# Attention strips loaded straight into the query and key tiles, the first group's one stage early, and products on idle TensorE whose results nobody reads

## The chip, the core and the metric

The kernel runs on one core of a Trainium2 chip, as one program. The metric is device time in microseconds (us), the median of several executions. The core has four compute engines, each with its own instruction queue: TensorE (PE, matrix products; PEld in the rows is its loading of weights), VectorE (DVE), ScalarE (ACT) and GpSimd (POOL). SyncE (SP) only issues DMAs here; ACT and POOL can issue them too. SBUF is the on-chip memory of 128 partitions, PSUM the eight banks into which TensorE writes. TensorE's clock has two levels, 1.2 and 2.4 GHz; the profile shows the granted clock as a share of the upper one (0.50 or 1.00).

## The reference

4096 tokens (8 sequences of 512) of width 128 pass through six residual steps. The part that the change touches is the fifth, windowed attention with 16 heads of width 8, and the mixture of experts before and after it:

```python
x = x + 0.5 * _L0_ffn_ref(_layernorm(x), ...)     # 8 experts, top 2
x = x + _L0_attn_ref(_layernorm(x), ...)          # a selective scan (Mamba)
x = x + 0.5 * _L0_ffn_ref(_layernorm(x), ...)
x = x + 0.5 * _L1_ffn_ref(_layernorm(x), ...)     # shared + 8 routed experts, top 1
x = x + _L1_attn_ref(_layernorm(x), ...)          # below
x = x + 0.5 * _L1_ffn_ref(_layernorm(x), ...)

def _L1_attn_ref(x, Wqkv, bqkv, Wout, bout):      # H = 16, WIN = 64, d = 8
    qkv = (x @ Wqkv.T + bqkv).reshape(B, S, 3, H, d).transpose(2, 0, 3, 1, 4)
    ...
    scores = jnp.einsum('bhncd,bhnld->bhncl', qc, kb) / np.sqrt(d)
    scores = jnp.where(band, scores, -jnp.inf)    # each query sees 64 keys
    attn = jax.nn.softmax(scores, axis=-1)
    o = jnp.einsum('bhncl,bhnld->bhncd', attn, vb)
    ...
    return o @ Wout.T + bout
```

## The kernel before

**Stages.** The program is a row of blocks with a barrier of all engines after each: `front` (the first three steps, woven together), `ffn1` with the tag `_f1`, `attention` (names ending in `_a`), and `ffn1` again with the tag `_f1b`. The residual stream stays in SBUF as `x_all`. In each block every engine has one instruction list, written out in Python and kept in that order; semaphores carry the dependences between engines.

**Products of high and low parts.** Operands are split into a part rounded to fp32r (`_hi`) and the rest (`_lo`), and `three` sums the three products that matter (L118 to L120 in the rows).

**ffn1.** A shared expert runs over 32 slots J (4 for each sequence): `shared_up` (six products into two PSUM banks), Gelu on ACT (`gel`, L1845), a multiplication on DVE (`hf`, L1854), `shared_down` two slots later (L1834). `EJ` = 24 slots come at the start, together with normalizing (`xn`), transposing (`xT`, L114), the gate (L1735) and the routing of each sequence; then 40 tiles of routed tokens; then the last slots, J from 24 to `AJ` - 1 = 31. The first block (`_f1`) also gets `opening`, functions of the attention stage that are run in it for sequence 0: loading the attention's weights, its norm, the transpose and the products for query, key and value (steps "T", "q", "k", "v" of `prep_pe`, `prep_act`, `prep_dve`), and the stores of queries and keys.

**Attention.** For each sequence the query and key, with their high and low parts, are written to DRAM (`q_rows`, `k_rows`: four copies of 8 rows for each head), so that a load can bring 32 rows, one head's products of both parts, under each other. A group is four heads (128 rows); there are 4 groups for each sequence, n = 0 to 31. `strips` loads a group's rows into `k_strips` and `q_strips`, two buffers each. ACT then copies the queries into `qd[n % 3]` (`set_queries`, four copies of 32 partitions), a tile in which each head's 32 rows have their own columns and the rest is zero, so that one product gives four heads' scores; DVE copies the keys into `kT[n % 3]` (`set_keys`). A query tile holds, for each block b of 32 queries, the 128 columns (head, query) next to each other:

```python
qd = [sb(f"qd{r}", [P, NB, HG, QB], F32R) for r in range(RQ)]
x = eng.matmul(BS[c][:, j * KW:(j + 1) * KW], qd[n % RQ][:, b, :, :].rearrange("p r q -> p (r q)"), kT[n % RQ][:, b * QB:b * QB + KW], ...)
```

The first operand of a product is the one that is loaded as weights, the second is streamed: a query block is the weights of a score product, 96 keys are streamed. A unit u is half a group, 8 blocks: there are 64. Each goes through `scores` (PE), `mask` and `find_max` (DVE), `less_max` (POOL), `exps` (ACT), `turn` (transposes on PE), `copy_p` (ACT), `weigh` (PE), `normalize` (DVE), `keep_own` (POOL) and `gather` (PE). PE runs them skewed: at turn t of its loop come `scores(t + 2)`, `turn(t)`, `weigh(t - 1)` and `gather(t - 2)`, and between them the steps that prepare the next sequence, by the table PLACES.

**Order at the start of attention.** PE waits for the first query and key tile; its order is `scores` of units 0, 1 and 2, the transpose "T" of sequence 1, then `turn(0)`. "T" needs `norm_out(1)` on ACT, and that `norm_root(1)` on POOL. POOL first sets all three `qd` tiles and the edges of `kT` to zero.

## Time and profile before

| | us |
|---|---|
| median of 3 executions | 1939.84 (1930.39 to 1942.37) |
| profiled execution, its device time | 1927.48 |
| its span, first to last instruction | 1925.7 |
| mean granted TensorE clock in it | 0.973 |
| block `_f1` begins | 1129.8 |
| block `attention` begins | 1367.2 |
| block `_f1b` begins | 1691.8 |

The span is the time in which the trace's rows lie, counted from 0. Most rows below are of the timeline: start, duration, engine, line, operation, output and inputs, count, and in brackets the idle time of the engine before it with what ended it. Rows of stretches give, for each engine, its busy time and number of instructions, then the granted clock (a share of the full one), the busy share of the 16 DMA engines and GB/s. "x16" with one duration means 16 instructions that follow one another.

### The profile page before, as it was taken

The page shows a single profiled execution, that of the slowest core. Times are in us where ns is not written, and L with a number is a line of the kernel's source. Part 1 is how long each engine was busy: PE and PEld are TensorE (multiplying, and loading weights), DVE is VectorE, ACT ScalarE, POOL GpSimd, SP SyncE. Part 2 cuts the span into 40 slices and gives each one's busy share as a digit, 9 for nine tenths or more (in the row PEclk, how much of TensorE's full clock was granted, in tenths as well). Part 3 has the DMA queues.
Part 4 walks back from the last instruction along what each step waited for, and adds up shares of the span by engine and source line. Part 5 has one row for each costly group of instructions (what it writes and reads, how often), then busy time and mean ns, then how long its engine had stood idle before and what let it go on. Part 6 is the DMA issues. An engine that isn't in the chain of part 4 may idle for free. (4 is left out here: it accounts for less than half of the span.)

```text
span 1925.7 us, 35660 instructions
## 1 busy us (share of the span) xinstructions
PE 1752.5 (91%) x12117; PEld 1506.5 (78%) x12117; DVE 1250.3 (65%) x2930; ACT 1103.0 (57%) x1935; POOL 1210.9 (63%) x1201
## 2 busy tenths in 40 slices
PE   7999898999999999887689989999699999989998
PEld 6878676787877778766477878888599999978886
DVE  2358789778787787978886436433567666656433
ACT  3466665766666766565555554343577767553442
POOL 3228687776877768778895725464656555534664
PEclk9999999999999999999889989999799999989999
DMA  4023332332333223332221401112554354101113
GB/s 145 1 69 113 92 107 87 108 97 86 102 91 109 94 84 108 91 101 78 78 99 55 117 14 44 38 46 67 156 160 127 116 154 137 39 24 35 46 45 108
DMA packets 120638, 166.95 MB, mean 87 GB/s; under 512 B 13878, under 2 KB 55820, under 8 KB 120460
## 3 DMA queue, kind: packets, MB, share of 16 engines
q1 hardware_dynamic: 112716, 147.74, 25.2%
q0 software_dynamic: 7168, 15.87, 2.7%
q8 instruction: 101, 1.65, 0.3%
q10 hardware_dynamic: 576, 1.05, 0.2%
q14 instruction: 77, 0.63, 0.1%
HBM read 114.28 MB, written 50.33 MB: 85 GB/s over the span
## 5 line engine op out<-in xcount | busy, mean ns | idle before, releaser
L777 POOL TENSOR_TENSOR db<-du_m,bt 128x512 f32<-128x512 f32 x256 | 328.5, 1284 | 137.6 <-DVE bank L782 136.7
L782 DVE TENSOR_TENSOR_SCAN bank<-bank,db 128x512 f32<-128x512 f32 x256 | 312.5, 1221 | 20.1 <-ACT bank L767 19.9
L808 POOL TENSOR_TENSOR y_m<-y_m,ph 128x512 f32<-128x512 f32 x240 | 313.4, 1307 | 0.4 <-DVE ph L797 0.4
L767 ACT ACTIVATE bank<-dt_m,a_neg 128x512 f32<-128x512 f32 x256 | 176.2, 688 | 96.6 <-DVE ph L797 90.0
L797 DVE TENSOR_TENSOR ph<-bank,ct 128x512 f32<-128x512 f32 x240 | 165.9, 691 | 11.2 <-POOL y_m L808 3.2
L1241 POOL TENSOR_TENSOR s_a<-s_a,mx_a 128x768 f32<-128x768 f32 x64 | 94.2, 1472 | 88.3 <-DVE mx_a L1349 88.2
L1380 PE MATMUL bank<-vb_a,pT_a 96*128 96x64 f32 x1024 | 121.5, 272 | 0.2 <-DVE o_a L1391 0.2
L1380 PEld LDWEIGHTS bank<-vb_a,pT_a 96*128 96x128 f32 x1024 | 119.4, 192 | 0.3 <-DVE o_a L1391 0.3
L354 PEld LDWEIGHTS bank<-dn,hf2b 128*128 128x128 f32 x680 | 91.3, 196 | 15.4 <-DVE x_all L413 5.7
L354 PEld LDWEIGHTS bank<-dn,hf1b 128*128 128x128 f32 x680 | 89.8, 193 | 11.2 <-DVE x_all L413 2.9
L354 PE MATMUL bank<-dn,hf2b 128*128 128x128 f32 x680 | 92.1, 280 | 6.5 <-DVE x_all L413 4.7
L354 PEld LDWEIGHTS bank<-dn,hf0b 128*128 128x128 f32 x688 | 90.3, 192 | 9.3 <-DVE x_all L413 1.0
L354 PEld LDWEIGHTS bank<-dn,hf2a 128*128 128x128 f32 x680 | 89.6, 193 | 8.5 <-DVE x_all L413 1.3
L354 PEld LDWEIGHTS bank<-dn,hf0a 128*128 128x128 f32 x688 | 90.3, 192 | 7.5
L354 PEld LDWEIGHTS bank<-dn,hf1a 128*128 128x128 f32 x680 | 89.0, 191 | 8.0 <-DVE x_all L413 0.6
L354 PE MATMUL bank<-dn,hf1b 128*128 128x128 f32 x680 | 90.7, 277 | 2.4 <-DVE x_all L413 2.0
L354 PE MATMUL bank<-dn,hf0b 128*128 128x128 f32 x688 | 91.1, 275 | 1.0 <-DVE x_all L413 0.6
L354 PE MATMUL bank<-dn,hf0a 128*128 128x128 f32 x688 | 90.8, 275 | 0.0
L354 PE MATMUL bank<-dn,hf2a 128*128 128x128 f32 x680 | 90.4, 276 | 0.4 <-DVE x_all L413 0.3
L354 PE MATMUL bank<-dn,hf1a 128*128 128x128 f32 x680 | 89.7, 275 | 0.2 <-DVE x_all L413 0.2
L385 ACT ACTIVATE hf1a<-bank,b 128x512 f32<-128x512 f32 x85 | 58.2, 685 | 53.6 <-PE bank L120 53.3
L1311 ACT CAST qd_a<-q_strips_a 32x512 fp32r<-32x512 f32 x128 | 78.7, 615 | 15.6 <-DMA q_strips_a<-q_rows 14.5
(458 smaller groups left out, 4864.9 us busy)
## 6 DMA issues: line engine op xcount, KB each, us to landing
bt<-bc_rows SPq DMA_DIRECT2D x128, 256.0 KB, 3.5
ct<-bc_rows SPq DMA_DIRECT2D x128, 256.0 KB, 3.4
sorted<-zero_row SPq DMA_DIRECT2D x64, 288.0 KB, 3.9
k_strips_a<-k_rows SPq DMA_DIRECT2D x32, 256.0 KB, 3.0
q_strips_a<-q_rows SPq DMA_DIRECT2D x32, 256.0 KB, 3.9
q_rows<-q_hi_a SPq DMA_DIRECT2D x16, 256.0 KB, 3.0
q_rows<-q_lo_a SPq DMA_DIRECT2D x16, 256.0 KB, 3.4
vb_a<-v_rows SPq DMA_DIRECT2D x16, 240.0 KB, 3.9
```

Of the source, the lines that this page charges most:

```text
L354: x = eng.matmul(Y.psum[:, t], hf[r][:, t], W["dn"][:, e, c, :], start=c == 0 and k == 0, stop=c == HC - 1 and k == NT - 1, skip_group_che ...
L385: eng.activation(hf[v % NR][:], HB[hbank(v)].psum[:], ACT.Relu, bias=W["b1"][:, e, c:c + 1]).then_inc(relu.sem)
L767: eng.activation(DH[J % 2][:], dt[s % 2][:, j % NH, :], ACT.Exp, scale=a_neg[:, j % NH, j // NH:j // NH + 1]).then_inc(da_done.sem)
L777: eng.tensor_tensor(db[J % RD][:], du[s % 2][:, j % NH, :], bt[N % RB][:], ALU.mult).then_inc(db_done.sem)
L782: eng.tensor_tensor_scan(DH[J % 2][:], DH[J % 2][:], db[J % RD][:], 0.0, ALU.mult, ALU.add).then_inc(hs_done.sem)
L797: eng.tensor_tensor(out, DH[J % 2][:], ct[N % RB][:], ALU.mult).then_inc(ph_done.sem)
L808: eng.tensor_tensor(y[s % 2][:, j % NH, :], y[s % 2][:, j % NH, :], ph[J % RP][:], ALU.add).then_inc(ys_done.sem)
L1241: eng.tensor_tensor(X[:], X[:], M[:, :, None].to_broadcast([P, UB, KW]), ALU.subtract).then_inc(sub_done.sem)
L1311: x = eng.copy(qd[n % RQ][p, :, r, :], q_strips[n % 2][p, :].rearrange("p (b q) -> p b q", q=QB))
L1380: x = eng.matmul(BO[:, at:at + 2 * GD], pT[u % 2][:, c * BB + j, :], vb[s % 2][:, b:NB + 1:NB - b, g * GD:(g + 1) * GD], start=True, stop= ...
```

## The change

1. **No copies into the tiles.** `q_strips`, `k_strips`, `set_queries` and `set_keys` go. `strips` now loads keys (one DMA of 128 partitions) and queries (four DMAs of 32 partitions, one for each head) straight into `kT[n % 3]` and `qd[n % 3]`; it waits until the scores of group n - 3 are done.
2. **Another layout of the queries.** Each head's queries are written in the order (query in block, block), so that a row stays contiguous for the DMA. The 128 weights of a score product are now every 16th element of 2048, 64 bytes apart, and ACT and DVE write the query parts with that stride (`by_block`).
3. **Sequence 0 is prepared one slot earlier** in `_f1`: "T", "q" and "k" move from slots J = 30, 31, 32 to 29, 30, 31. Its stores are split between ACT (high keys) and SP (the rest), and the first group's strips are loaded in `_f1`, into tiles whose memory `ffn1` no longer uses then; POOL zeroes them there (`clear_group(0)`).
4. **POOL's order at the start of attention** changes: group 1's tile, `vb`, `less_max(0)`, group 2's tile, `norm_root(1)`, `less_max(1)`, `bias_out(0)`.
5. **Products that nobody reads** (`warm`, 128 x 512 each, into a free bank): 8 at the start of each `ffn1` and 7 more after its first transposes, 24 at the end of `_f1`, 4 at the start of attention.

```diff
+def warm(eng, psum, tile, n):
+    for _ in range(n):
+        eng.matmul(psum[:], tile[:, 0, 0:P], tile[:, 0, :], start=True, stop=True)
...
         def prep_act(eng, s, name):
...
-                eng.activation(hi[:], X[:], ACT.Identity, bias=b_cols[:, col:col + 1]).then_inc(pa.sem)
+                eng.activation(by_block(hi, name), X[:].rearrange("p (b q) -> p b q", q=QB), ACT.Identity, bias=b_cols[:, col:col + 1]).then_inc(pa.sem)
...
+        def by_block(tile, name):
+            return tile[:].rearrange("p (q b) -> p b q", b=NB) if name == "q" else tile[:].rearrange("p (b q) -> p b q", q=QB)
...
+        def strips(eng, s, g, keys=True, heads=range(HG)):
+            n = s * HG + g
+            if g == 0:
+                eng.wait_ge(q_out.sem, q_out.at(s, "last"))
+                eng.wait_ge(k_out.sem, k_out.at(s, "last"))
+            q, ld = qd[n % RQ], strip_in[n % RQ]
+            if n >= RQ:
+                eng.wait_ge(sc_done.sem, sc_done.at(2 * (2 * (n - RQ) + 1) + 1))
+            else:
+                eng.wait_ge(zeroed.sem, zeroed.at(0, f"qd{n}"))
+            if keys:
+                eng.dma_start(kT[n % RQ][:, PAD:PAD + SEQ].bitcast(F32), k_rows[s, HG * g:HG * g + HG].rearrange("r c d t -> (r c d) t")).then_inc(ld.sem, 16)
+            for h in heads:
+                eng.dma_start(q[32 * h:32 * h + 32, h, :].bitcast(F32), q_rows[s, HG * g + h].rearrange("c d t -> (c d) t")).then_inc(ld.sem, 16)
...
-            eng.dma_start(k_strips[n % 2][:], k_rows[s, heads].rearrange("r c d t -> (r c d) t")).then_inc(strip_in[n % 2].sem, 16)
-            eng.dma_start(q_strips[n % 2][:], q_rows[s, heads].rearrange("r c d t -> (r c d) t")).then_inc(strip_in[n % 2].sem, 16)
...
-                x = eng.matmul(BS[c][:, j * KW:(j + 1) * KW], qd[n % RQ][:, b, :, :].rearrange("p r q -> p (r q)"), kT[n % RQ][:, b * QB:b * QB + KW], start=True, stop=True)
+                x = eng.matmul(BS[c][:, j * KW:(j + 1) * KW], qd[n % RQ][:].rearrange("p h (q b) -> p (h q) b", b=NB)[:, :, b], kT[n % RQ][:, b * QB:b * QB + KW], start=True, stop=True)
...
@@ ffn1: sync, act @@
             if opening:
                 opening["store_queries"](eng, 0)
+                opening["store_low_keys"](eng, 0)
+                opening["strips"](eng, 0, 0, heads=(0, 1))
...
             if opening:
-                for name in ("q", "k"):
-                    opening["prep_act"](eng, 0, name)
-                opening["store_keys"](eng, 0)
+                opening["prep_act"](eng, 0, "k")
+                opening["store_high_keys"](eng, 0)
+                opening["strips"](eng, 0, 0, keys=False, heads=(2, 3))
...
@@ ffn1: pe @@
+            warm(eng, HB[3].psum, up_hi[0], 8)
...
                 turns(v)
+                if v == -1:
+                    warm(eng, HB[3].psum, up_hi[0], 7)
                 gates(v)
...
-                if opening and J >= AJ - 2:
-                    opening["prep_pe"](eng, 0, ("T", "q", "k", "v")[J - AJ + 2])
+                if opening and J in (AJ - 3, AJ - 2, AJ - 1, AJ + 1):
+                    opening["prep_pe"](eng, 0, {AJ - 3: "T", AJ - 2: "q", AJ - 1: "k", AJ + 1: "v"}[J])
+            if opening:
+                HB[0].wait(eng)
+                warm(eng, HB[0].psum, up_hi[0], 24)
```

How this moves instructions is seen at three places. The first is ACT at the end of `_f1` and the start of attention; `gel_f` are the last slots' Gelus. Before:

```order
L1845 ACTIVATE gel_f<-bank 128x512 [waits f1_shared_up,f1_shared_hidden]
L1175 ACTIVATE q_hi_a<-bank,b_cols_a 128x512 [waits a_prep_pe,a_bias_dve]
L1175 ACTIVATE k_hi_a<-bank,b_cols_a 128x512 [waits a_prep_pe,a_bias_dve]
L1075 DMA k_rows<-k_hi_a 16x8x512 [waits a_prep_dve]
L1075 DMA k_rows<-k_hi_a 16x8x512
L1075 DMA k_rows<-k_lo_a 16x8x512 x2
L2090 UNCONDITIONAL_BRANCH
L1492 UNCONDITIONAL_BRANCH [waits barrier_Pool_Activation_PE_DVE_SP_release]
L1311 CAST qd_a<-q_strips_a 32x16x32 [waits a_strips0_in,a_zeroed]
```

Now:

```order
L1188 ACTIVATE q_hi_a<-bank,b_cols_a 128x16x32 [waits a_prep_pe,a_bias_dve]
L1847 ACTIVATE gel_f<-bank 128x512 [waits f1_shared_up,f1_shared_hidden]
L1188 ACTIVATE k_hi_a<-bank,b_cols_a 128x512 [waits a_prep_pe,a_bias_dve]
L1079 DMA k_rows<-k_hi_a 16x8x512 [waits a_prep_act]
L1079 DMA k_rows<-k_hi_a 16x8x512
L1216 DMA qd_a<-q_rows 32x512 [waits a_zeroed,a_k_stored,a_q_stored]
L1216 DMA qd_a<-q_rows 32x512
L2097 UNCONDITIONAL_BRANCH
L1490 UNCONDITIONAL_BRANCH [waits barrier_Pool_Activation_PE_DVE_SP_release]
L1359 ACT_TABLE_LOAD
```

The query's high part has moved ahead of the last Gelu, two of the key stores have gone to SP, and two strip loads, which wait for all stores, now stand before the barrier; the copies after it are gone. The second place is POOL at the start of attention. Before (`s_a` is the `less_max` of units 0 to 3):

```order
L1256 MEMSET qd_a 128x2048 x3
L87 TENSOR_SCALAR sd_a<-mv_a 128x4 [waits a_norm_dve]
L96 TENSOR_SCALAR nm_a<-mv_a 128x4
L90 TENSOR_TENSOR rs_a<-sd_a,minus_half 128x4 [waits a_norm_pool]
L100 TENSOR_TENSOR nm_a<-nm_a,rs_a 128x4 [waits a_norm_pool]
...
L1236 TENSOR_TENSOR x_all<-x_all,b_all_a 128x512 [waits a_bias_dve,a_prep_act]
L1241 TENSOR_TENSOR s_a<-s_a,mx_a 128x768 [waits a_max_done] x4
```

Now:

```order
L1223 MEMSET qd_a 128x2048
...
L1271 TENSOR_TENSOR s_a<-s_a,mx_a 128x768 [waits a_max_done]
L1221 MEMSET kT_a 128x32
L1222 MEMSET kT_a 128x32
L1223 MEMSET qd_a 128x2048
L87 TENSOR_SCALAR sd_a<-mv_a 128x4 [waits a_norm_dve]
L96 TENSOR_SCALAR nm_a<-mv_a 128x4
L90 TENSOR_TENSOR rs_a<-sd_a,minus_half 128x4 [waits a_norm_pool]
```

The norm of sequence 1 (`rs_a`, `nm_a`) stood ahead of the first `less_max` and now stands behind it and behind one more zeroing. The third is PE at the same border (L1834, now L1836, is `shared_down`). Before:

```order
L1154 MATMUL bank<-xT_a,w_k_a 128x512 [waits a_prep_act]
L1834 MATMUL bank<-k_dn,hf_f 128x128 [waits f1_shared_hidden]
L1834 MATMUL bank<-k_dn,hf_f 128x128 x3
L1158 MATMUL bank<-w_v_a,xT_a 128x128 [waits a_prep_dve]
L1158 MATMUL bank<-w_v_a,xT_a 128x128 x3
L2090 UNCONDITIONAL_BRANCH
L1494 UNCONDITIONAL_BRANCH [waits barrier_Pool_Activation_PE_DVE_SP_release]
L1335 MATMUL bank<-kT_a,qd_a 128x96 [waits a_keys_set,a_queries_set]
```

Now:

```order
L1163 MATMUL bank<-xT_a,w_k_a 128x512 [waits a_prep_act]
L1836 MATMUL bank<-k_dn,hf_f 128x128 [waits f1_shared_hidden]
L1836 MATMUL bank<-k_dn,hf_f 128x128 x3
L1836 MATMUL bank<-k_dn,hf_f 128x128 [waits f1_shared_hidden]
L1836 MATMUL bank<-k_dn,hf_f 128x128 x3
L1167 MATMUL bank<-w_v_a,xT_a 128x128 [waits a_prep_dve]
L1167 MATMUL bank<-w_v_a,xT_a 128x128 x3
L120 MATMUL bank<-k_up_hi 128x512 [waits f1_shared_hidden]
L120 MATMUL bank<-k_up_hi 128x512 x23
L2097 UNCONDITIONAL_BRANCH
L1492 UNCONDITIONAL_BRANCH [waits barrier_Pool_Activation_PE_DVE_SP_release]
L120 MATMUL bank<-k_up_hi 128x512 x4
```

The key product stands one `shared_down` (two rows) earlier, and 24 + 4 unread products stand on the two sides of the barrier.

## Rows read from the trace of the kernel before

**Rows 1.** The page, busy time of TensorE: share of the span, instructions.

```profile
PE 1752.5 (91%) x12117; PEld 1506.5 (78%) x12117; DVE 1250.3 (65%) x2930; ACT 1103.0 (57%) x1935; POOL 1210.9 (63%) x1201
```

**Rows 2.** Stretches: the attention once it runs.

```profile
1390.00:1660.00 270.00, 267.27 (x2847) 252.91 (x2847) 188.77 (x451) 194.46 (x331) 153.06 (x156) 1.00 0.46 137
```

**Rows 3.** All waits of PE from 1384 to 1660 us: total, times, longest.

```profile
PE bank L1289 <- ACT oT_a L1296: 2.7, 7, 0.4
```

**Rows 4.** Timeline, attention, one unit: scores, turn, the next scores.

```profile
1663.85 0.97 PEld L1335 LDWEIGHTS bank<-kT_a,qd_a 128*128 128x128 f32 x8
...
1664.76 0.83 PEld L1361 LDWEIGHTS bank<-ident,s_a 128*96 128x96 f32 x8
...
1668.12 0.97 PEld L1335 LDWEIGHTS bank<-kT_a,qd_a 128*128 128x128 f32 x8
```

**Rows 5.** Timeline, `_f1`: streamed products of 512 columns at clock 1.00.

```profile
1342.49 0.39 PE L118 MATMUL bank<-xT_hi_f,k_up_hi 128*128 128x512 f32 x1
...
1342.72 0.40 PE L119 MATMUL bank<-xT_lo_f,k_up_hi 128*128 128x512 f32 x1
```

**Rows 6.** The page, groups by cost: busy, mean ns, idle before them.

```profile
L1311 ACT CAST qd_a<-q_strips_a 32x512 fp32r<-32x512 f32 x128 | 78.7, 615 | 15.6 <-DMA q_strips_a<-q_rows 14.5
```

**Rows 7.** Timeline, the end of `_f1`: the low part of the keys.

```profile
1359.21 0.74 DVE L1184 SCALAR_TENSOR_TENSOR k_lo_a<-bank,b_cols_a,k_hi_a 128x512 fp32r<-128x512 f32 x1
```

**Rows 8.** Stretches: the border to attention, and where the clock is back.

```profile
1362.00:1364.00 2.00, 0.00 (x0) 0.00 (x0) 0.00 (x0) 0.00 (x0) 0.00 (x0) 0.98 0.95 290
...
1384.00:1386.00 2.00, 2.00 (x12) 1.46 (x12) 1.33 (x3) 1.98 (x5) 0.58 (x1) 0.90 0.00 0
```

**Rows 9.** Timeline, the start of attention.

```profile
1367.22 0.34 SPq L1206 DMA_DIRECT2D k_strips_a<-k_rows  x1
...
1367.52 5.57 POOL L1256 MEMSET qd_a<- 128x2048 f32 x3
...
1370.73 2.50 ACT L1311 CAST qd_a<-q_strips_a 32x512 fp32r<-32x512 f32 x4 [12.35 <-DMA q_strips_a<-q_rows]
...
1373.18 0.23 POOL L87 TENSOR_SCALAR sd_a<-mv_a 128x4 f32<-128x4 f32 x1
1373.28 3.59 PEld L1335 LDWEIGHTS bank<-kT_a,qd_a 128*128 128x128 f32 x16 [12.31 <-ACT qd_a L1311]
...
1374.80 0.20 POOL L100 TENSOR_TENSOR nm_a<-nm_a,rs_a 128x4 f32<-128x4 f32 x1
...
1377.06 1.46 POOL L1241 TENSOR_TENSOR s_a<-s_a,mx_a 128x768 f32<-128x768 f32 x1
...
1379.31 1.63 ACT L104 ACTIVATE xn_a<-x_all,nm_a,rs_a 128x128 f32<-128x128 f32 x4
...
1381.12 0.71 PEld L114 LDWEIGHTS bank<-ident,xn_a 128*128 128x128 f32 x4
```

**Rows 10.** Stretches: the start of `_f1`.

```profile
1132.00:1140.00 8.00, 6.11 (x19) 4.85 (x19) 2.39 (x8) 4.62 (x9) 3.54 (x20) 0.50 0.09 25
```

**Rows 11.** Timeline, the start of `_f1` on TensorE.

```profile
1131.52 0.89 PE L114 MATMUL bank<-ident,xn_f 128*128 128x128 f32 x4 [3.17 <-ACT xn_f L1756]
...
1134.30 0.79 PE L118 MATMUL bank<-xT_hi_f,k_up_hi 128*128 128x512 f32 x1 [1.89 <-DVE xT_lo_f L1778]
...
1141.92 0.25 PEld L118 LDWEIGHTS bank<-xT_hi_f,k_up_hi 128*128 128x128 f32 x1
```

**Rows 12.** Timeline, the start of `_f1b` on TensorE.

```profile
1693.48 1.12 PE L114 MATMUL bank<-ident,xn_f1b 128*128 128x128 f32 x4 [2.72 <-ACT xn_f1b L1756]
...
1696.49 0.79 PE L118 MATMUL bank<-xT_hi_f1b,k_up_hi 128*128 128x512 f32 x1 [1.89 <-DVE xT_lo_f1b L1778]
...
1697.08 0.63 PE L119 MATMUL bank<-xT_lo_f1b,k_up_hi 128*128 128x512 f32 x1
...
1697.51 0.63 PE L120 MATMUL bank<-xT_hi_f1b,k_up_lo 128*128 128x512 f32 x1
...
1705.45 0.39 PE L118 MATMUL bank<-xT_hi_f1b,k_up_hi 128*128 128x512 f32 x1
```

More of the change, by code:

```diff
@@ L1070, in store_queries, with store_high_keys, store_low_keys @@
                 eng.dma_start(q_rows[s, :, copy, :, :], (q_hi, q_lo)[copy % 2][:].bitcast(F32)).then_inc(q_out.sem, 16)
-        def store_keys(eng, s):
+        def store_high_keys(eng, s):
+            eng.wait_ge(pa.sem, pa.at(s, "k"))
+            for copy in (0, 1):
+                eng.dma_start(k_rows[s, :, copy, :, :], k_hi[:].bitcast(F32)).then_inc(k_out.sem, 16)
+        def store_low_keys(eng, s):
             eng.wait_ge(pd.sem, pd.at(s, "k"))
-            for copy in range(4):
-                eng.dma_start(k_rows[s, :, copy, :, :], (k_hi, k_lo)[copy // 2][:].bitcast(F32)).then_inc(k_out.sem, 16)
+            for copy in (2, 3):
+                eng.dma_start(k_rows[s, :, copy, :, :], k_lo[:].bitcast(F32)).then_inc(k_out.sem, 16)
         def load_weights(eng):
@@ L1183, in prep_dve @@
                 eng.wait_ge(pa.sem, pa.at(s, name))
-                eng.scalar_tensor_tensor(lo[:], X[:], b_cols[:, col:col + 1], hi[:].bitcast(F32), ALU.add, ALU.subtract).then_inc(pd.sem)
+                eng.scalar_tensor_tensor(by_block(lo, name), X[:].rearrange("p (b q) -> p b q", q=QB), b_cols[:, col:col + 1],
+                                         by_block(hi, name).bitcast(F32), ALU.add, ALU.subtract).then_inc(pd.sem)
             elif name == "v":
@@ new lines, in clear_group @@
+        def clear_group(eng, r):
+            eng.memset(kT[r][:, 0:PAD].bitcast(F32), 0.0)
+            eng.memset(kT[r][:, PAD + SEQ:].bitcast(F32), 0.0)
+            eng.memset(qd[r][:].bitcast(F32), 0.0).then_inc(zeroed.sem)
+        with ExitStack() as ahead:
+            tiles = [[ahead.enter_context(nc.sbuf_tensor(f"{name}{r}_a", [P, *shape], F32R)) for name, shape in (("qd", (HG, SEQ)), ("kT", (PADDED,)))]
+                     for r in range(RQ)]
+        qd, kT = [t[0] for t in tiles], [t[1] for t in tiles]
@@ L1190, in attention @@
+        yield dict(load_weights=load_weights, store_queries=store_queries, store_high_keys=store_high_keys, store_low_keys=store_low_keys, strips=strips, clear_group=clear_group, set_ones=set_ones, set_masks=set_masks, biases_pe=biases_pe, biases_dve=biases_dve,
                    norm_stats=norm_stats, norm_root=norm_root, norm_out=norm_out, prep_pe=prep_pe, prep_act=prep_act, prep_dve=prep_dve)
-        qd = [sb(f"qd{r}", [P, NB, HG, QB], F32R) for r in range(RQ)]
-        kT = [sb(f"kT{r}", [P, PADDED], F32R) for r in range(RQ)]
@@ L1194, in attention @@
-        q_strips, k_strips = two("q_strips", [P, SEQ]), two("k_strips", [P, SEQ])
+        sb("groups", [P, RQ * (HG * SEQ + PADDED)])
         vb = two("vb", [KW, NB + 1, D])
@@ L1212, in sync @@
                     store_queries(eng, s)
-                    store_keys(eng, s)
-                eng.wait_ge(q_out.sem, q_out.at(s, "last"))
-                eng.wait_ge(k_out.sem, k_out.at(s, "last"))
-                strips(eng, s, 0)
+                    store_high_keys(eng, s)
+                    store_low_keys(eng, s)
+                    strips(eng, s, 0)
                 strips(eng, s, 1)
@@ L1250, in pool @@
         def pool(eng):
-            for r in range(RQ):
-                eng.memset(kT[r][:, 0:PAD].bitcast(F32), 0.0)
-                x = eng.memset(kT[r][:, PAD + SEQ:].bitcast(F32), 0.0)
-            x.then_inc(zeroed.sem)
-            for r in range(RQ):
-                eng.memset(qd[r][:].bitcast(F32), 0.0).then_inc(zeroed.sem)
-            norm_root(eng, 1)
+            clear_group(eng, 1)
             for p in range(2):
@@ L1262, in pool @@
             x.then_inc(zeroed.sem)
+            less_max(eng, 0)
+            clear_group(eng, 2)
+            norm_root(eng, 1)
+            less_max(eng, 1)
             bias_out(eng, 0)
-            for u in range(2):
-                less_max(eng, u)
             for t in range(NU + 1):
@@ L1405, in pe @@
         def pe(eng):
+            warm(eng, BT[0], K["up_hi"][0], 4)
             for u in range(2):
@@ L1449, in act @@
                             prep_act(eng, s + 1, name)
-                if t % 2 == 0 and t + 4 < 2 * NG:
-                    set_queries(eng, t // 2 + 2)
             project_act(eng, NSEQ - 1)
@@ L1477, in dve @@
                             prep_dve(eng, s + 1, name)
-                if t % 2 == 0 and t + 4 < 2 * NG:
-                    set_keys(eng, t // 2 + 2)
                 if k == 4 and 1 <= s < NSEQ:
@@ L2074, in dve @@
             for J in range(EJ, AJ + 2):
+                if opening and J in (AJ - 1, AJ):
+                    opening["prep_dve"](eng, 0, ("q", "k")[J - AJ + 1])
                 if J < AJ:
@@ L2080, in dve @@
                     opening["biases_dve"](eng)
-                if opening and J == AJ - 4:
+                if opening and J == AJ - 5:
                     eng.wait_ge(added.sem, added.at(FINAL.index(0)))
                     opening["norm_stats"](eng, 0)
-                if opening and J == AJ:
-                    opening["prep_dve"](eng, 0, "q")
             if opening:
-                for name in ("k", "v"):
-                    opening["prep_dve"](eng, 0, name)
+                opening["prep_dve"](eng, 0, "v")
         with nc.Block() as block:
```

46 lines of the change are left out of this document (9 added, 37 removed).

## The prediction

> **What bounds the kernel now.** I read the page first: TensorE is busy for 91% of the span [rows 1], more than any other engine, so the question at each place is whether TensorE waits there. Then the stretches and the waits of the attention. Once it runs, TensorE is busy for 267.27 of 270 us at a clock of 1.00 [rows 2], and all that it waits for is 2.7 us behind a copy of ACT [rows 3]. ACT and DVE are busy for 194 and 189 of those 270 us: they have room. So time that is taken from ACT or DVE there buys nothing, and time that is added to a product is paid in full. The reader is to see in [rows 4] how such a unit passes: 8 score products start at 1663.85, the transposes at 1664.76, the next unit's scores at 1668.12, a period of 4.27 us with no gap.
>
> TensorE does wait at the borders of the stages, so I read these in the timeline. At the start of attention it waits for 12.31 us until the first strips are in their tiles [rows 9]. And behind each border its clock is low: 0.50 from 1132 to 1140 [rows 10], and still 0.90 on average in 1384 to 1386, 17 us after attention began [rows 8]. There products take about twice as long: 0.43 us from 1697.08 to 1697.51 against 0.23 us at clock 1.00 [rows 12, 5].
>
> **The copies (nothing).** 128 copies on ACT, 78.7 us [rows 6], and 32 on DVE go. All but the first group's stand beside a TensorE that does not wait, so they return nothing; at most the 2.7 us of [rows 3], which are waits for another copy of ACT. In their place come 160 DMAs instead of 64 on SP's queue, for the same bytes. They wait for the scores of group n - 3 and are needed two groups, 4 units or 17 us, later. A first strip load took 3.5 us from issue to use (1367.22 to 1370.73, [rows 9]); with five issues of some 0.4 us it is 5 to 6. Also behind a sequence's eight stores it has about three units, 13 us. That cover hides it; without it each group would add up to 5 us, 160 us in all, and I see nothing that takes the cover away.
>
> **The strided weights (0, up to +55 us).** Each of the 512 score products now loads 128 weights that lie 64 bytes apart. No row shows a strided weight load, so I bound it by its neighbours. Contiguous, 8 products take 0.91 us [rows 4], 0.114 each. They stream only 96 columns, which at the rate of [rows 5] (0.23 us for 512) is 0.043 us: the loading of weights sets their pace, at 0.89 ns a weight. The streamed side passes an element in 0.45 ns, so that reading of SBUF can go twice as fast as weights are loaded. If the stride halves the fastest reading, weights still come at 0.90 ns and the cost is nil. If it halves the weights' own rate, each load costs another 0.107 to 0.114 us: 512 x 0.107 = +55 us, with nothing to hide it. Below nothing there is no case: the same 128 weights are loaded. I take 0, because the weight load uses half the rate that the streamed rows show, and keep +55 as the far end.
>
> The Trainium skill has a rule against this layout (SBUF — State Buffer, section Door 1: The DMA port swizzle): SBUF lines are 16 bytes, full speed needs at least two hits in a line, and an access that goes to a new line each time pays a penalty. Here every weight is in a line of its own; before, four shared one. The page gives no size of the penalty, and no row of this trace shows it; by the rule the sum is that of the second rival, without it the forecast's.
>
> ACT and DVE write the query parts with the same stride, 8 times each. Bounded by a doubling of about 0.7 us each this is 11 us of work on engines with room; on the path it stands once, for sequence 0, +0 to +1.4 us.
>
> **The start of attention (-1.7 us, from -5 to +2).** Sequence 0's keys come one slot earlier. A slot is some 2.3 us (six products at 0.23 and four f32 products of about the same together), but the low keys wait on DVE and ACT for the last Gelu and the query's part now, so I take 1.9: the low part ends at 1358.1 instead of 1359.95 [rows 7]. The stores are bound by the DMA engines (share 0.95 at 290 GB/s, [rows 8]), all eight start 1.9 us earlier, and so have landed by about 1365.2 instead of 1367.1. Then come the strips, 3.5 us, and no copy of 2.50 us: scores may begin at 1368.7 instead of 1373.28, -4.6 us. But scores are not what TensorE is late for. It becomes busy for good with the transpose "T" at 1381.12, and ahead of it stands now a longer chain. From the first score to POOL's start on unit 0 it was 3.8 us at most (1373.28 to 1377.06, with another operation of POOL ahead), I take 3.3 from 1368.7, to 1372.0; POOL's `less_max(0)` 1.46, to 1373.5; zeroing of a tile 5.57/3 = 1.86 and its edges 0.2, to 1375.5; `norm_root(1)` 1373.18 to 1375.00, 1.82, to 1377.3; `norm_out(1)` on ACT 1.63, to 1379.0; "T" at 1379.1. That is -2.0. If the barrier waits for ACT's own strip loads to land (before, it opened when the last store must have landed), attention begins at 1368.8, DVE has its norm statistics to do first, and "T" comes at 1379.8, -1.3. I take the middle, -1.7. What is late next is thus POOL's chain, not the strips. The bounds: -5 if the strips alone counted; +2 if a strided write, the barrier and POOL all go against it.
>
> The 24 products at the end of `_f1` take 24 x 0.23 = 5.5 us from 1359.2 and end before the barrier opens, so they cost nothing. I give them nothing either: before, the clock was 0.98 on average in 1362 to 1364 [rows 8] after the last weight load at 1361.0 (1373.28 less the 12.31 idle), so it fell near 1364; now it may hold until about 1367.5, and between then and "T" TensorE has long gaps again (two units of scores are 1.9 us of work). The time in which it came back, 1381 to 1385, stays.
>
> **The start of `_f1` (-3.0 us, from -4 to 0).** TensorE is free from 1129.8; its transposes come at 1131.52 [rows 11]. Eight products of 0.23 us end at 1131.7, so they delay it by 0.1 to 0.2. Seven more end at 1134.0, before the first real product at 1134.30. If TensorE is thus busy enough, the clock doesn't fall, and the work from 1134.30 to 1141.92 (12 products of `three`, 8 of the gate, 4 transposes) passes at clock 1.00: 12 x 0.23 + 8 x 0.11 = 3.7 us against 7.6. But the transposes there need ACT's `gel` and `xn`, 2.3 us behind the first six products, at about 1138.2, so that the next slot begins at 1138.7 instead of 1141.92: -3.2, less the 0.2. TensorE is then busy without waits to speak of, so what is gained stays.
>
> **The start of `_f1b` (-1.8 us, from -3 to +2.5).** Here the clock is low when the block begins at 1691.8. Eight products at 0.43 us end at 1695.2, and the transposes, ready at 1693.48 [rows 12], wait for them: +1.7. The seven end at 1698 to 1699.1, and the first real product moves from 1696.49 by 1.7 to 2.6. In return the clock rises earlier. Before, it was back by 1705.45, 9.0 us after dense work began. Dense work now begins at 1691.8, so it is back by 1700.8, or by 1697 if the some 4 us of attention (1381.12 to 1385) hold. Real work done at 1705.45 was worth 4.5 us at clock 1.00; now it is done at 1704.4 or 1702.7: -1.0 or -2.7, middle -1.8.
>
> **Sum.** 0 + 0 - 1.7 - 3.0 - 1.8 = -6.5 us on the profiled execution (1927.48 to 1921.0). That execution lies 12.4 us below the median of the three runs; the same difference from the median, 1939.84, is 1933.3. The runs lie 12 us apart: about 1% is what a measurement of this kernel can tell from no change.
>
> **Rivals.** (a) *The clock isn't held.* The unread products don't keep or bring back the clock, as in `_f1b`, where it stayed low through 8 us of dense work. Then only their delays are left: +0.2 in `_f1`, +2.6 in `_f1b`, and -1.7 in attention: +1.1, 1941. For it: the same 8 us. Against it: it did come back in each case, and in `_f1` it need only not fall. Chance 0.2. (b) *Strided weights are slow*, slower than before: one mechanism, at L1341, 512 times. It decides from 0.05 us a load (26 us less the 6.5 of the rest is +1%); at +0.107 it gives 1939.8 + 55 - 6.5 = 1988. For it: the products are bound by loading weights, and nothing covers it [rows 2, 4]. Against it: the rate of [rows 5]. Chance 0.15, with half of it below 1965. (c) *ACT and DVE were the hidden bound.* If relief brings TensorE's products closer together, by 0.3 us in each of 64 units, it is -19 and more, 1914. Against it stands [rows 3]. Chance 0.04.
>
> **How the numbers follow.** Forecast 0.61, (a) 0.2, (b) 0.15, (c) 0.04. Within 1%: 0.81, the first two. Slower: 0.15. Faster by over 1%: 0.04. The forecast alone spans 1939.8 - 12 to 1939.8 + 4.5 by its bounds, some 5 us more on each side for the scatter of the medians. The range goes from 1921 to 1958: it leaves out (c) below, and the larger part of (b) above.
>
> **What would show it.** In the attention stretch: PEld pitch of L1341 at 0.114 us and a unit of 4.27 us; if it is 5.1 us, (b). At the start: first scores near 1368.7, then a gap of TensorE, ended by "T", whose releaser is ACT's `xn_a` and behind it POOL; if "T" comes before 1377, my chain is wrong. In `_f1`: clock 1.00 from 1132 to 1140 and the third slot near 1138.7. In `_f1b`: transposes near 1695.2, clock back by 1700. What would make the prediction wrong: a price on the strided weights, strips that land late in the middle of attention (TensorE waits for a strips DMA at L1341), or a barrier that holds attention back.

## The result: 152 us slower, and the profile after

The changed kernel takes 2091.31 us (median of 4 runs, 2083.93 to 2097.41) against 1938.99 for the kernel before (4 runs beside them): a ratio of 1.0791, with a 95% interval of 1.0740 to 1.0842. The forecast was 1933 us, and its range ended at 1958. In the experiments below one execution of e10 (4690 us) and one of e12 (3442 us) stand far off all others of their kernels and count in none of the medians and ratios. The profiled execution has a span of 2087.2 us, 161.5 more than the 1925.7 of before.

The page of the kernel after: the busy time, the line of granted clocks in 40 slices, and two groups of weight loads.

```profile
PE 1924.9 (92%) x12175; PEld 1668.8 (80%) x12175; DVE 1246.6 (60%) x2898; ACT 1037.3 (50%) x1807; POOL 1206.6 (58%) x1201
...
PEclk9999999999999999989999999986556666599999
...
L1386 PEld LDWEIGHTS bank<-vb_a,pT_a 96*128 96x128 f32 x1024 | 177.0, 268 | 0.7 <-DVE o_a L1397 0.3
...
L1341 PEld LDWEIGHTS bank<-kT_a,qd_a 128*128 128x128 f32 x512 | 117.2, 310 | 5.7 <-DMA qd_a<-q_rows 1.6
```

TensorE is as busy as in [rows 1], 92%, with 58 products more, and yet for 172 us longer. The clock line shows where: nine slices in the attention stand at 5 to 8 tenths. It is not only the scores (L1341) that got dearer: L1386, the weighing of values, whose weights did not change their place, went from 192 to 268 ns a load. From the start of the first scores to the start of the last eight it is now 459.8 us (1370.1 to 1829.9) against 299.1 (1373.3 to 1672.4): 160.7 us, the whole loss.

Stretches of the kernel after (busy us of PE, PEld, DVE, ACT and POOL, then the granted clock), to be held against [rows 2]:

```profile
1400.00:1500.00 100.00, 100.00 (x677) 95.45 (x676) 42.83 (x100) 32.31 (x53) 35.10 (x38) 0.64 0.28 80
1500.00:1700.00 200.00, 200.00 (x1344) 187.27 (x1345) 90.01 (x204) 65.81 (x105) 70.86 (x74) 0.66 0.31 90
...
1564.00:1580.00 16.00, 16.00 (x150) 15.00 (x148) 8.80 (x16) 7.08 (x12) 6.14 (x6) 0.99 0.66 201
1584.00:1624.00 40.00, 40.00 (x237) 37.99 (x237) 15.53 (x44) 11.39 (x19) 13.69 (x16) 0.50 0.13 37
```

TensorE never waits here, 100.00 of 100 us, and its clock is nevertheless 0.50, the lower level of 1.2 GHz, for most of the time: a mean of 0.65 between 1.00 and 0.50 means 70% of the time at 0.50. It changes about once in a sequence of 8 units: some 40 us low, some 16 us high. The copies that are gone freed ACT and DVE; nothing came of it.

The timeline of TensorE at either level (start, duration, one row for a run of like products):

```profile
1481.18 2.00 PE L1341 MATMUL bank<-kT_a,qd_a 128*128 128x96 f32 x8
1482.98 1.93 PE L1367 MATMUL bank<-ident,s_a 128*96 128x128 f32 x8
...
1489.14 2.00 PE L1341 MATMUL bank<-kT_a,qd_a 128*128 128x96 f32 x8
...
1506.54 1.96 PE L1341 MATMUL bank<-kT_a,qd_a 128*128 128x96 f32 x8
1508.33 1.12 PE L1315 MATMUL bank<-w_o_a,oT_a 128*128 128x128 f32 x8
```

Take starts, not durations. At clock 1.00 eight scores take 1.79 us (1506.54 to 1508.33), twice the 0.91 of [rows 4]. At 0.50 they take 1.80 (1481.18 to 1482.98), nearly what contiguous weights took at that clock ([rows 9], 3.59 us for 16). So the time of these loads, 64 bytes apart, does not follow TensorE's clock. A whole unit at 0.50 is 7.96 us (1481.18 to 1489.14).

### The profile page after: what moved, and what is told of

It is laid out like the page before. It is cut to its first block and busy times, and to the rows that moved or that the text cites. A ratio compares the mean times of both kernels' runs of the same rounds, so it can differ in the third digit from the quotient of the medians.

```text
span 2087.2 us, 35618 instructions
## 1 busy us (share of the span) xinstructions
PE 1924.9 (92%) x12175; PEld 1668.8 (80%) x12175; DVE 1246.6 (60%) x2898; ACT 1037.3 (50%) x1807; POOL 1206.6 (58%) x1201
## 5 line engine op out<-in xcount | busy, mean ns | idle before, releaser
L1386 PEld LDWEIGHTS bank<-vb_a,pT_a 96*128 96x128 f32 x1024 | 177.0, 268 | 0.7 <-DVE o_a L1397 0.3
L1386 PE MATMUL bank<-vb_a,pT_a 96*128 96x64 f32 x1024 | 177.0, 348 | 0.2 <-DVE o_a L1397 0.2
L1374 ACT COPY pT_a<-bank 96x512 f32<-96x512 f32 x128 | 72.6, 584 | 180.3 <-PE bank L1367 180.1
L1278 POOL TENSOR_TENSOR o_a<-o_a,own_a 128x256 f32<-128x256 f32 x64 | 46.6, 728 | 143.3 <-DVE o_a L1397 143.3
L1341 PE MATMUL bank<-kT_a,qd_a 128*128 128x96 f32 x512 | 126.6, 408 | 1.6 <-DMA qd_a<-q_rows 1.2
L1341 PEld LDWEIGHTS bank<-kT_a,qd_a 128*128 128x128 f32 x512 | 117.2, 310 | 5.7 <-DMA qd_a<-q_rows 1.6
L1350 DVE SCALAR_TENSOR_TENSOR s_a<-bank,band_a 128x384 f32<-128x384 f32 x128 | 71.1, 557 | 77.8 <-PE bank L1341 77.3
L1393 DVE RECIPROCAL rc_a<-bank 128x8 f32<-128x8 f32 x64 | 13.3, 208 | 161.2 <-PE bank L1386 161.2
L1367 PE MATMUL bank<-ident,s_a 128*96 128x128 f32 x512 | 103.5, 371 | 0.0
```

What stands on the lines that cost most here:

```text
L1341: x = eng.matmul(BS[c][:, j * KW:(j + 1) * KW], qd[n % RQ][:].rearrange("p h (q b) -> p (h q) b", b=NB)[:, :, b], kT[n % RQ][:, b * QB:b * ...
L1350: eng.scalar_tensor_tensor(sc[u % 4][:, c * BB:(c + 1) * BB, :], BS[c][:, 0:BB * KW].rearrange("p (b k) -> p b k", k=KW), scale, band[:, N ...
L1367: x = eng.transpose(BT[c][0:KW, j * P:(j + 1) * P], sc[u % 4][:, c * BB + j, :], C["ident"][:])
L1374: eng.copy(pT[u % 2][:, c * BB:(c + 1) * BB, :].rearrange("p b q -> p (b q)"), BT[c][0:KW, :]).then_inc(pT_done.sem)
L1386: x = eng.matmul(BO[:, at:at + 2 * GD], pT[u % 2][:, c * BB + j, :], vb[s % 2][:, b:NB + 1:NB - b, g * GD:(g + 1) * GD], start=True, stop= ...
```

## The experiments

Where nothing else is said, a time is from one execution and is given as the difference from the kernel before on the same chip. The chips differ (medians of 1932 to 1962 us for the same kernel), so the difference is what counts. Executions of the kernel before on one chip lie 13 to 23 us apart, so a single difference of less than that is not told from 0. e3 has 10 executions, e9 13, e10 and e12 11, e11 12 and e16 8; for these the ratio to before with its interval is given. The changed kernel stands at +152.

### The stride, put in alone and taken out alone

e1 is the kernel before, with only this:

```diff
-  qd[n % RQ][:, b, :, :].rearrange("p r q -> p (r q)")
+  qd[n % RQ][:].rearrange("p b r q -> p (b r q)").rearrange("p (c s) -> p c s", s=NB)[:, :, b]
```

> The kernel before, with one thing changed: the weights of the 512 score products are read 16 elements (64 bytes) apart in the query tile that the copies have set, so the scores are of the wrong queries and the output is not the reference's; the number of instructions and of columns is the same. Theory 1 (the stride alone makes the whole loss, by doubling the load and by taking the granted clock with it): about 1939 + 150 = 2090 us, 8 scores in 1.74 us at clock 1.00, and the clock falls to 0.50 for most of the attention. Theory 2 (the stride doubles the load and no more; the clock falls for another reason, such as the copies that are gone): 512 x 0.104 = 53, about 1992 us, clock about 1.00 in the attention. Theory 3 (the stride costs nothing by itself): 1939 us.

e2 is the kernel after, with only this:

```diff
-  qd[n % RQ][:].rearrange("p h (q b) -> p (h q) b", b=NB)[:, :, b]
+  qd[n % RQ][:].rearrange("p h t -> p (h t)")[:, b * P:(b + 1) * P]
```

> The changed kernel, with one thing changed: the score products read their 128 weights contiguous, so the scores are of a wrong mixture of queries and the output is not the reference's; everything else, the interleaved tiles, the five strip loads and the unread products, is as in the changed kernel. Theory 1: the time comes back to the sum of the other edits, 1939 - 6 = 1933 us (1925 to 1940). Theory 2: 2091 - 53 = about 2038 us, with the clock still at 0.50 for most of the attention. Theory 3: 2091 us.

Measured: e1 2084.1 us, +149.9; e2 1934.9 us, +0.7. Theory 1 holds from both sides: the distance between the weights makes the whole loss, the fall of the clock included, and all the other edits together make nothing that one run can tell. In e1, timeline at clock 1.00:

```profile
1414.62 1.96 PE L1335 MATMUL bank<-kT_a,qd_a 128*128 128x96 f32 x8
1416.41 1.06 PE L1361 MATMUL bank<-ident,s_a 128*96 128x128 f32 x8
...
1419.75 1.52 PE L1335 MATMUL bank<-kT_a,qd_a 128*128 128x96 f32 x6
```

A unit takes 5.13 us (1414.62 to 1419.75) instead of 4.27. So at clock 1.00 the loads alone are worth 64 x 0.86 = 55 us, the far end of my bounds to the us. The other 105 of the 160.7 are the remainder, and the clock is what is left to make them: at 0.50 a unit takes 7.96 us in the kernel after.

### How far apart is too far

e6, e15, e5 and e8 are e1 with a distance of 2, 3, 4 and 8 elements in place of 16 (`s=2` and so on, with blocks chosen to stay in the tile).

> The kernel before, with the score weights read 2 elements (8 bytes) apart; the scores are of the wrong queries. Theory 1a: a contiguous load's 0.114 us each and 1939 us. Theory 1b: 0.218 each and about 2084 us. Anything between would say that the load's time follows the distance, and would show whether the granted clock falls already with a load that is only partly slower.

> The kernel before, with the score weights read 3 elements (12 bytes) apart, between 8 bytes (1945 us, load as contiguous) and 16 bytes (2102 us, load doubled); the scores are of the wrong queries. If the load needs two of its elements in each 16 bytes: 12 bytes apart, 4 in 3 such pieces, it is partly slow, 0.114 x 1.5 = 0.17 us each, some 1970 us, more if the clock falls. If only distances up to 8 bytes are fast: 0.218 each and 2100 us.

> The kernel before, with the score weights read 4 elements (16 bytes) apart instead of side by side; the scores are of the wrong queries. Theory 1a (the load slows in steps with the distance, and 64 bytes is at the slow end): 8 scores between 0.91 us (the contiguous 0.114 each) and 1.74 us at clock 1.00, and the clock falls only if the load is slow; 1939 us with a load of 0.114, 2000 to 2085 us with a slower one. Theory 1b (any distance above 4 bytes costs the full doubling): 0.218 each and 2084 us, as with 64 bytes.

> The kernel before, with the score weights read 8 elements (32 bytes) apart; the scores are of the wrong queries. Theory 1a: between the time of 16 bytes apart and that of 64, 2000 to 2084 us. Theory 1b: 0.218 us each and 2084 us.

Measured, with the time of 8 scores at clock 1.00 from the start of their first product to the next start behind them, and the mean clock in 1400 to 1660, where all six are inside the attention. ([rows 4], by the starts of the weight loads, had 0.91 for before; by the starts of the products it is 0.93.)

| bytes apart | 8 scores, us | clock | against before |
|---|---|---|---|
| 4 (before) | 0.93 | 1.00 | 0 |
| 8 (e6) | 0.98 | 1.00 | -1.3 |
| 12 (e15) | 1.44 | 0.75 | +91.5 |
| 16 (e5) | 1.90 | 0.75 | +155.8 |
| 32 (e8) | 1.94 | 0.69 | +173.2 |
| 64 (e1) | 1.79 | 0.70 | +149.9 |

Three timelines for it, of before, of e6 and of e5, all at clock 1.00:

```profile
1402.99 1.10 PE L1335 MATMUL bank<-kT_a,qd_a 128*128 128x96 f32 x8
1403.92 1.06 PE L1361 MATMUL bank<-ident,s_a 128*96 128x128 f32 x8
```

```profile
1405.51 1.15 PE L1335 MATMUL bank<-kT_a,qd_a 128*128 128x96 f32 x8
1406.49 1.06 PE L1361 MATMUL bank<-ident,s_a 128*96 128x128 f32 x8
```

```profile
1414.41 2.07 PE L1335 MATMUL bank<-kT_a,qd_a 128*128 128x96 f32 x8
1416.31 1.06 PE L1361 MATMUL bank<-ident,s_a 128*96 128x128 f32 x8
```

Neither theory had it whole. The load slows in steps (1a), but 16 bytes are already the slow end, not the middle, and 64 bytes are a little faster than 32. Two weights in 16 bytes cost next to nothing (0.05 us in eight), four in 48 bytes make 1.5 times, one in 16 bytes doubles. At clock 0.50 the eight take 1.91 us in e5 (1419.66 to 1421.57) and 1.95 in e8 (1423.02 to 1424.97), as at 1.00. The Trainium skill (SBUF — State Buffer, section Door 1: The DMA port swizzle) asks for at least two hits in a line of 16 bytes; these rows agree with that for weight loads (0.98 us with two weights in a line, 1.90 with one), and give the size that the page leaves out.

### What takes the clock

e13 and e14 have no stride. They are the kernel before with a second, unread product behind each score, with the same contiguous weights and 8 or 96 columns:

```diff
   x = eng.matmul(BS[c][:, j * KW:(j + 1) * KW], qd[...], kT[n % RQ][:, b * QB:b * QB + KW], ...)
+  x = eng.matmul(BS[c][:, BB * KW:BB * KW + 8], qd[...], kT[n % RQ][:, b * QB:b * QB + 8], ...)
```

> The kernel before, weights contiguous; after each score product an unread one with the same 128x128 weights and 8 columns of keys, into the part of the bank that nobody reads: 512 more loads of 0.114 us at clock 1.00, with next to no columns. Theory A (the clock falls where loads take the time and few columns move, whatever makes the loads long): the clock falls as with the strided weights, to 0.65 to 0.80 in the attention, and the time is 2060 to 2120 us. Theory B (the clock falls because the weights are read strided): clock 1.00 and 1939 + 512 x 0.114 = 1997 us.

> As the run with 8 columns, but 96 columns each: the same 512 extra loads and nearly the same time at clock 1.00, with 12 times the columns. Theory A: the clock stays higher than with 8 columns, 1.00 if columns are what counts, and the time is 1939 + 512 x 0.115 = 1998 us. Theory B: clock 1.00, 1998 us. If this run too falls to half clock, it is the share of loads and not the columns.

Measured: e13 2208.4 us, +253; e14 2003.0 us, +47.6. The same stretch of both, e13 first:

```profile
1400.00:1700.00 300.00, 300.00 (x2051) 284.17 (x2051) 123.67 (x280) 131.03 (x219) 96.89 (x98) 0.64 0.27 82
```

```profile
1400.00:1700.00 300.00, 300.00 (x3071) 285.41 (x3071) 180.38 (x428) 186.43 (x316) 142.95 (x148) 0.99 0.40 120
```

The two kernels have the same loads, and while the clock is 1.00 a pair takes the same 0.22 us in both. Only the columns differ, and with 8 the clock goes to 0.64 on average, with 96 it stays. That is theory A, and B is out as the only cause: the clock can be lost with contiguous weights, by loads with few columns behind them. TensorE is 100% busy in both, so busy time doesn't tell it. e13 even loses more than the stride did, beyond the expected 2120, because its contiguous extra loads slow with the clock: eight pairs take 3.43 us there (1508.44 to 1511.87).

e4 and e7 go at it from the other side: the kernel after, its stride kept, with one or two unread products of 512 columns ahead of each half of the turns.

```diff
             if u >= 1:
                 eng.wait_ge(pT_done.sem, pT_done.at(2 * (u - 1) + c))
+            warm(eng, BT[c], K["up_hi"][0], 1)
             for j in range(BB):
```

> The changed kernel with one unread product of 128x512 ahead of each half of the turns, 128 in all, into the bank that the turns overwrite; the strided weights stay. If strided loads leave the array too thin and that takes the clock: it holds 1.00 in the attention, a unit takes 4.27 + 0.83 + 2 x 0.23 = 5.6 us, and the time is about 1939 + 64 x 1.3 - 6 = 2016 us, below the changed kernel although work is added. If the clock falls for another reason: 2091 + 128 x 0.23 to 0.46 = 2120 to 2150 us.

> The changed kernel with two unread products of 128x512 ahead of each half of the turns, 256 in all (one each, 128 in all, gave 2059 us and a clock of 0.86 in the attention). If strided loads leave the array too thin and more columns hold the clock: 1.00 in the attention, a unit of 4.27 + 0.83 + 4 x 0.23 = 6.0 us, 1939 + 64 x 1.75 - 6 = 2045 us, below 2059 with 128 products more. If the columns don't matter to the clock: 2059 + 128 x 0.23 to 0.46 = 2090 to 2120 us.

Measured: e4 2058.8 us, +124.6, mean clock 0.89 in 1500 to 1700; e7 2076.6 us, +130.7, clock 0.93. Adding 128 products whose results nobody reads made the kernel some 27 us faster. But my numbers were wrong: the clock rose and was not held, and the second 128 gained nothing that one run can tell. So columns are not the whole condition. Before, a unit streams 3328 columns in 4.27 us (scores, turns, weighing and gathering); in e7 it streams 5376 in 6.11 us (1585.32 to 1591.43, at clock 1.00), which is more in each us, and its clock still falls. Why so many columns beside the scores don't hold it, when e14's among them do, stays open; that the stride has an effect on the clock of its own, beside making the loads longer, is not excluded.

### The unread products at the borders

e12 is the kernel before with the 8 and the 7 products at the start of either sparse FFN; e3, told below, is the kernel after with contiguous weights, and e11 is e3 without these 15; e10 is e3 without the 24 and the 4 at the seam into attention.

```diff
             expert = {}
+            warm(eng, HB[3].psum, up_hi[0], 8)
             for v in SLOTS:
...
                 turns(v)
+                if v == -1:
+                    warm(eng, HB[3].psum, up_hi[0], 7)
```

> The kernel before with only the 8 and 7 unread products at the start of either sparse FFN added. The forecast's value: 4.8 us less than before, 1934 us where before has 1939, ratio 0.9975. Rival: nothing, ratio 1.000.

> The version with contiguous weights, without the 8 and the 7 unread products at the start of either sparse FFN. The forecast's value: they are worth 3.0 us in the first and 1.8 in the second, so 1929.3 + 4.8 = 1934 us. Rival: they are worth nothing, 1929 us.

> The version with contiguous weights, without the 24 and the 4 unread products at the seam into the attention. The forecast's value: nothing is lost, 1929 us, since the clock falls before the first real work in any case. Rival: without them the first scores and the turns of the attention run at 0.50, 16 scores 3.6 us instead of 2.1 us, 1 to 4 us more.

Measured: e12 1927.9 us where before has 1932.2, 0.9976 of before (0.9957 to 0.9995), some 5 us. e11 is 1.0013 of before (0.9990 to 1.0035) and e3, on another chip, 0.9977 (0.9953 to 1.0000): some 7 us between them, with an uncertainty of some 6 from the two intervals. Both have the forecast's direction and size, and neither fixes it closer. Timeline of `_f1` in the kernel after, against [rows 11]:

```profile
1133.45 2.08 PE L120 MATMUL bank<-k_up_hi 128*128 128x512 f32 x8 [1.49 <-PEq L1007]
1135.38 0.60 PE L114 MATMUL bank<-ident,xn_f 128*128 128x128 f32 x4
1135.73 1.86 PE L120 MATMUL bank<-k_up_hi 128*128 128x512 f32 x7
1137.86 0.50 PE L123 MATMUL bank<-xT_hi_f,k_up_hi 128*128 128x512 f32 x1 [0.27 <-DVE xT_lo_f L1780]
...
1142.16 0.48 PE L123 MATMUL bank<-xT_hi_f,k_up_hi 128*128 128x512 f32 x1
```

The 1.89 us of idling ahead of the first real product are 0.27, and from there to the third slot it takes 4.30 us instead of 7.7 (1134.30 to 1141.99). The front ended 3.6 us later in this execution, so I measure from the front's last product group: 11.26 us (1130.90 to 1142.16) against 14.70 (1127.29 to 1141.99), -3.4. In e12 at `_f1b`, from the last projection to the third slot, it is 13.92 us (1691.09 to 1705.01) against 15.50 (1688.69 to 1704.19), -1.6.

e10 came to 0.9983 of before (0.9964 to 1.0002), e3, on another chip, to 0.9977: 1 us, which these intervals don't resolve from nothing. In e10's profiled execution the first 16 scores ran at 0.50 and "T" came 21.6 us after the low keys begin; in e3's the first 16 ran at 1.00 and "T" came after 20.9. But e9, told below, has the 24 products too, and in its profiled execution the first scores ran at 0.50 as well.

### A version that beats both

e3 keeps the direct loads and writes the contiguous layout with them, in runs of 128 bytes (`by_block` then leaves the queries in their natural order, as it does the keys):

```diff
-  (("qd", (HG, SEQ)), ...
+  (("qd", (NB, HG, QB)), ...
-  eng.dma_start(q[32 * h:32 * h + 32, h, :], q_rows[s, HG * g + h].rearrange("c d t -> (c d) t"))
+  eng.dma_start(q[32 * h:32 * h + 32, :, h, :], q_rows[s, HG * g + h].rearrange("c d (b q) -> (c d) b q", q=QB))
-  qd[n % RQ][:].rearrange("p h (q b) -> p (h q) b", b=NB)[:, :, b]
+  qd[n % RQ][:, b, :, :].rearrange("p r q -> p (r q)")
```

> The changed kernel with its outputs as the reference has them, and contiguous weights: queries are stored in their natural order, and each strip's load puts its 16 runs of 32 elements (128 bytes) where the copies had put them. Theory 1: about 1933 us, if the loads in pieces of 128 bytes stay hidden; a group then lands later than in the changed kernel, where 4.1 us went from issue to the first scores, and each us more at the attention's start is 1 us of the time. Theory 2: about 2038 us. A rival inside theory 1: the pieces make the first group's strips late by 5 to 10 us, about 1940 us.

e9 moves `norm_root(eng, 1)` ahead of `less_max(eng, 0)` in GpSimd's program, and e16 adds unread products in the gaps that are left at the start of attention:

```diff
-            warm(eng, BT[0], K["up_hi"][0], 4)
+            warm(eng, BT[0], K["up_hi"][0], 8)
             for u in range(2):
                 for c in range(2):
                     scores(eng, u, c)
+            warm(eng, BT[0], K["up_hi"][0], 8)
             for t in range(NU + 2):
...
                     scores(eng, t + 2, 1)
+                if t == 0:
+                    warm(eng, BT[0], K["up_hi"][0], 5)
```

> The version with strips loaded in pieces of 128 bytes and contiguous weights (1929.3 us, 0.9977 of before), and in GpSimd's program of the attention norm_root(1) ahead of less_max(0) and clear_group(2). It waits for nothing there, its 1.82 us end before the maxima are there, and ScalarE's normalizing pass then starts at the end of the exps (1372.7) instead of 1375.7: 3.0 us less, 1926 us. Rival: the clock, which is at 0.50 there, comes back later for it or the strips of the second group end last, and nothing is gained (1929).

> The version with contiguous weights and norm_root(1) first (1925.3 us, 0.9964 of before), with unread products in the gaps of the attention's start too: 8 instead of 4 ahead of the first scores, 8 between group 0's and group 1's scores, 5 ahead of the first transposes. If the gaps are what loses the clock there: it stays 1.00 from the sparse FFN into the attention, the 4 us of work at half clock behind the first transposes pass in 2, and the time is 1925 - 2 to 4 us, more below in executions in which the clock came back late. If it is lost all the same, 21 products at 0.43 us delay the start by 1 to 4 us: 1926 to 1929.

Measured: e3 1929.3 us where before has 1934.2, 0.9977 of it (0.9953 to 1.0000); e9 1925.3 us where before has 1932.2, 0.9964 (0.9945 to 0.9984); e16 1946.2 us where before has 1961.8, 0.9914 (0.9881 to 0.9947). These are three chips. e3's interval ends at 1 and overlaps e9's, so the step from e3 to e9 is not resolved; e16's just touches e9's. e3's stretch, against [rows 2]:

```profile
1390.00:1660.00 270.00, 267.26 (x2847) 252.91 (x2846) 175.41 (x420) 129.56 (x218) 148.41 (x155) 1.00 0.54 131
```

TensorE does 2847 products in 267.26 us, as it did with the copies; ACT has 65 us less to do (129.56 for 194.46) and nothing is gained. The runs of 128 bytes stay hidden. The chain at e3's start:

```profile
1365.82 1.81 POOL L1223 MEMSET qd_a<- 128x2048 f32 x1
...
1372.41 1.94 PE L1341 MATMUL bank<-kT_a,qd_a 128*128 128x96 f32 x8 [2.40 <-DMA qd_a<-q_rows]
...
1375.72 1.65 ACT L104 ACTIVATE xn_a<-x_all,nm_a,rs_a 128x128 f32<-128x128 f32 x4 [3.00 <-POOL nm_a L100]
...
1377.42 1.12 PE L114 MATMUL bank<-ident,xn_a 128*128 128x128 f32 x4 [3.07 <-ACT xn_a L104]
```

"T" waits for ACT's `xn_a`, and ACT waits 3.00 us for POOL. With POOL's order changed (e9), "T" comes 18.7 us after the low keys begin, not 20.9. In these gaps the clock falls: here 0.50 in 1372 to 1380. In e9's profiled execution it stayed down long into dense work:

```profile
1385.00:1410.00 25.00, 24.26 (x113) 21.49 (x113) 10.11 (x18) 9.97 (x17) 10.62 (x9) 0.50 0.70 178
1415.00:1440.00 25.00, 25.00 (x273) 23.88 (x269) 16.52 (x39) 12.38 (x22) 13.54 (x16) 1.00 0.35 73
```

From the low keys to the last scores that execution took 322.6 us, e3's 312.0. e16, which fills the gaps:

```profile
1370.00:1374.00 4.00, 2.83 (x13) 2.01 (x11) 0.00 (x0) 0.00 (x0) 0.00 (x0) 1.00 0.49 133
1374.00:1378.00 4.00, 3.24 (x8) 2.60 (x9) 1.58 (x10) 1.28 (x1) 3.12 (x11) 0.60 0.62 115
1378.00:1382.00 4.00, 3.72 (x25) 3.24 (x24) 3.02 (x6) 0.00 (x0) 2.35 (x4) 0.97 0.84 192
1382.00:1386.00 4.00, 3.65 (x26) 3.01 (x25) 2.81 (x4) 2.59 (x6) 4.00 (x6) 1.00 0.58 165
```

The clock still dips, while the eight products behind the barrier run, but it is back with the first scores and stays through "T", and from the low keys to the last scores it is 309.3 us. So with the gaps filled the work of the attention's start runs at full clock, as the first theory of that run had it in kind, though not "it stays 1.00". That a clock lost in the gaps is what made the 24 products worthless is the likely reading; it is not shown, since e16 was not run without them. Against before, e16 gains 15.5 us where 9 to 11 were expected. Its trace has 2.7 us of that against e3's: "T" comes 19.6 us after the low keys for 20.9, and from "T" to the last scores it is 289.8 us for 291.1. That trace is of e16's fastest execution (1933.5 us), and there is none of before on that chip; what the rest of the gain is stays open.

## Why the prediction was wrong, point by point

**The strided weights (0, up to +55 us): this step failed, twice, and it alone makes the miss.** First in the value I took. I argued that the streamed side passes an element in 0.45 ns, so that halving it leaves the weights' 0.90 ns as they are. e1 and e5 show that a weight load has a limit of its own: with one weight in 16 bytes it takes 0.22 to 0.24 us at either clock. The rate at which columns stream says nothing about that. Second in the far end. +55 was right for the loads (5.13 us a unit against the 5.1 of rival (b)) but not a bound, because it held the clock at 1.00. I had read [rows 2], clock 1.00 with TensorE dense, and [rows 10 and 12], clock low where it had been idle, and took it, without saying so in the prediction, that a busy TensorE keeps its clock. e13 against e14 shows that a TensorE that is 100% busy can lose it when its loads have few columns behind them, and e4 and e7 that columns are not the whole condition. So rival (b) had the first half of the mechanism, the dearer load, and lacked the second, the clock: its 1988 was 103 us short. With the stride out and the rest in, e3 stands at 0.9977 of before, -4.4 us, where the sum had -6.5.

**The copies (0): right.** e2 and e3; 65 us less on ACT in the stretch of [rows 2], 267.26 us of TensorE as before.

**The start of attention (-1.7): small, and half right.** From `_f1`'s third slot to "T" it was 239.1 us before, 238.6 after and 236.2 in e3: -0.5 and -2.9. POOL's chain was late next, as forecast, and the barrier did not wait for the strips (TensorE went on at 1367.7, the strips came at 1370.1). From the third slot to the low keys it was 217.2, 216.6 and 215.3 us, so the 1.9 us that I took for an earlier start came in e3 alone. The strided writes of the query parts took 1.17 and 1.13 us for 0.69 and 0.75 (ACT, DVE), 0.9 us of what after lacks against e3, and from the first score to POOL's `less_max(0)` it was 3.65 us (3.3 forecast) for e3's 2.85, 0.8 more; the rest I can't assign from single executions.

**The 24 products (0): not told from 0** by e10; e16 suggests what they lack, work up to the first scores and between them.

**`_f1` (-3.0) and `_f1b` (-1.8): right**, -3.4 and -1.6 by the trace, and 0.9976 for both by e12. Rival (a) falls with them. In `_f1b` the 8 products took 3.55 us, at half clock, as costed, and the clock was back for the first real product.

**Rival (c)** has nothing for it: ACT and DVE relieved, same pitch.

## What to carry to other kernels

Removing work from an engine with room was worth nothing here, and paying for it on the engine that bounds cost 150 us: a layout that saves copies puts the bill on each weight load. Keep at least two 32-bit weights in each 16 bytes (0.98 us for eight products against 1.90); if a layout must be rearranged, let the DMA do it (runs of 128 bytes were hidden here). When costing anything that lengthens TensorE's weight loads or thins its columns, cost the kernel at half clock as well, and when filling idle time with unread products, fill it up to the dense work: behind 28 such products and gaps of 0.6 to 1.8 us the first scores ran at 0.50 in e9 and at 1.00 in e3, and "T" at 0.50 in both; with the gaps filled (e16) both ran at 1.00, by one trace each.
